# Attention with a gated feed-forward part: 70 products on a zero tile during the first loads, and another order of the first loads, splits and transposes

## What is computed

```python
xn = layernorm(x)                                  # over the last axis, no scale
s  = attn(xn)      # 16 heads of 128 over 4 key/value heads, causal softmax, output product,
                   # bias, gelu, + xn, layernorm with gamma and beta
gate_up = xn @ w_gate_up.T                         # 256 -> 2 x 1024
gate, up = split(gate_up, 2)
g  = silu((silu(gate) * up) @ w_down.T)            # 1024 -> 256
out = x + s * g
```

## Time and profile before

| | us |
|---|---|
| median of 3 runs | 727.29 |
| lowest, highest | 726.42, 732.52 |
| span of the profiled execution, from its first to its last instruction | 725.2 |

### The profile page before, as it was taken

The page is one execution under the profiler, slowest core; times in us unless marked ns, Lnnn a source line. Parts: engine busy times, 40 slices in busy tenths (PEclk is TensorE's granted clock), DMA queues, the critical chain, the costliest instruction groups (busy, mean ns, idle before and its releaser), DMA issues.

```text
span 725.2 us, 13208 instructions
## 1 busy us (share of the span) xinstructions
PE 679.8 (94%) x4032; PEld 594.3 (82%) x4032; DVE 493.0 (68%) x1636; ACT 428.5 (59%) x1011; POOL 280.1 (39%) x328
## 2 busy tenths in 40 slices
PE   2799999999899999999899999999999999999993
PEld 1678888888788888898788888887888898888872
DVE  6955433335777777778668677776777778867777
ACT  2423233326666667677667676866667677767671
POOL 2499100000523324157615142583324157615234
PEclk9699999999999999999999999999999999999998
DMA  8334000002000000000200000002000000200000
GB/s 273 116 117 145 1 29 0 30 0 88 1 1 2 1 1 1 1 1 1 91 2 1 2 1 1 2 4 89 1 1 1 1 1 1 88 1 2 0 1 30
DMA packets 14522, 20.52 MB, mean 28 GB/s; under 512 B 752, under 2 KB 12144, under 8 KB 14192
## 3 DMA queue, kind: packets, MB, share of 16 engines
q1 hardware_dynamic: 13328, 14.37, 6.0%
q0 software_dynamic: 1120, 5.24, 2.2%
HBM read 15.41 MB, written 4.19 MB: 27 GB/s over the span
## 4 chain that ended last, share of the span: by engine, by line
PE 84%; DVE 7%; ACT 3%; issue 3%; DMA 1%; SPq 0%; POOL 0%; DVEq 0%; ACTq 0%
PE bank L941 40%; PE down_ps L941 34%; PE down_ps L1028 8%; PE bank L1015 2%; DVE cT_lo L808 2%; ACT cT_hi L690 2%; DVE hidT_lo L754 1%; DMA raw<-in_wgu 1%; PE bank L994 1%; ACT probs L681 1%; DVE xnT_lo L739 1%; DVE pT_lo L792 1%; DVE xn L731 0%; DVE stats L716 0%; ACT wgu_hi L593 0%
## 5 line engine op out<-in xcount | busy, mean ns | idle before, releaser
L551 POOL TENSOR_TENSOR probs<-probs,inv 128x512 f32<-128x512 f32 (+3 forms) x256 | 181.1, 721 | 390.9 <-DVE inv L892 390.7
L681 ACT ACTIVATE probs<-probs,least 128x512 f32<-128x512 f32 (+3 forms) x256 | 142.4, 558 | 46.5 <-DVE least L885 45.0
L885 DVE CUSTOM_DVE_ANT_0 probs<-bank,mask 128x512 f32<-128x512 f32 (+3 forms) x256 | 121.4, 487 | 11.7 <-issue 11.2
L687 ACT ACTIVATE pT_hi<-down_ps 128x512 fp32r<-128x512 f32 x156 | 92.7, 594 | 49.1 <-PE down_ps L1028 41.8
L792 DVE TENSOR_TENSOR pT_lo<-down_ps,pT_hi 128x512 fp32r<-128x512 f32 x156 | 107.0, 686 | 17.4 <-ACT pT_hi L687 14.3
L1028 PE MATMUL down_ps<-ident,probs 128*128 128x128 f32 x624 | 93.5, 272 | 2.3 <-POOL probs L551 2.3
L1028 PEld LDWEIGHTS down_ps<-ident,probs 128*128 128x128 f32 x624 | 75.4, 140 | 14.8 <-POOL probs L551 2.5
L941 PE MATMUL down_ps<-wo_lo,cT_hi 128*128 128x256 f32 x256 | 73.5, 287 | 4.1 <-DVE cT_lo L808 3.0
L803 DVE SCALAR_TENSOR_TENSOR qT_lo<-bank,bias,qT_hi 128x512 fp32r<-128x512 f32 x64 | 47.7, 749 | 41.2 <-ACT qT_hi L671 41.2
L941 PE MATMUL bank<-kT_lo,qT_hi 128*128 128x512 f32 (+2 forms) x192 | 70.3, 366 | 2.4 <-issue 2.4
L941 PE MATMUL down_ps<-wo_hi,cT_lo 128*128 128x256 f32 x256 | 72.1, 282 | 0.0
(11 more groups left out here) (136 smaller groups left out, 1603.3 us busy)
## 6 DMA issues: line engine op xcount, KB each, us to landing
x_row<-in_x SPq DMA_DIRECT2D x4, 512.0 KB, 6.8
raw<-in_wgu SPq DMA_DIRECT2D x4, 512.0 KB, 6.0
raw<-in_wq POOLq DMA_DIRECT2D x2, 1024.0 KB, 5.2
raw<-in_wo POOLq DMA_DIRECT2D x2, 1024.0 KB, 6.4
g_scratch<-g_out SPq DMA_DIRECT2D x4, 512.0 KB, 2.9
x_b<-in_x SPq DMA_DIRECT2D x4, 512.0 KB, 3.6
g_b<-g_scratch SPq DMA_DIRECT2D x4, 512.0 KB, 4.6
out<-res SPq DMA_DIRECT2D x3, 512.0 KB, 3.5
```

The lines of the kernel that those rows point to most:

```text
L551: nc.gpsimd.tensor_tensor(p, p, inv[:, u % UNITS, g:g + 1].to_broadcast([P, (tile_of(u) + 1) * P]), ALU.mult).then_inc(probs_made, 1)
L681: nc.scalar.activation(p, p, ACT.Exp, bias=least[:, u % UNITS, g:g + 1], scale=-1.0, accum_out=total[:, u % UNITS, g:g + 1]).then_inc(exp_ ...
L687: nc.scalar.activation(hi[:], ps, ACT.Copy).then_inc(probsT_hi, 1)
L885: nc.vector.tensor_tensor_reduce(out=probs[t][:, g, :], in0=ps[:, 0:(t + 1) * P], in1=mask[:, (T - 1 - t) * P:], scale=-SCALE, scalar=BIG, ...
```

## The change

- TensorE: after a wait for a new zeroed tile `clock` (128x128 fp32r, a memset on VectorE), 70 matmuls of that tile with itself into the first 128 columns of bank 3. Nothing reads the result.
- SP: piece 0 of the gate/up weights and then the identity stand ahead of x of row 1.
- POOL: the low part of weight part 1 stands ahead of the root of row 1.
- ScalarE: silu of gate (0,0) stands ahead of the high parts of row 1.
- VectorE: the statistics of row 1 stand behind normalising row 0, the low part of weight part 0 and the low parts of row 0. The rest is in the order shown in the diff.
- TensorE: gate_up(0, 0) waits for the low parts of row 0 only, and stands ahead of the transposes of row 1. These now go to banks 1 and 3, and a wait for their low parts stands ahead of gate_up(0, 1).

```diff
+CLOCK_RUNS = 70
@@ build
+    clock = sb("clock", [P, P], F32R)
-    xT_ps = [flat[0:2], flat[2:4],
+    xT_ps = [flat[0:2], [flat[1], flat[3]],
              [down_ps[:, 0, :], down_ps[:, 1, :]], [down_ps[:, 2, :], down_ps[:, 3, :]]]
@@ sync
         load_tokens(0)
+        load_piece(0)
+        sp.dma_start(ident[:], ident_in).then_inc(ident_loaded, 16)
         load_tokens(1)
-        sp.dma_start(ident[:], ident_in).then_inc(ident_loaded, 16)
-        load_piece(0)
         load_tokens(2)
@@ gpsimd
         root1(0)
+        ffn_low(POOL_PARTS[0])
         root1(1)
-        ffn_low(POOL_PARTS[0])
         root1(2)
         root1(3)
@@ scalar
         ffn_high(0, 1)
         xT_high(0)
+        gate_part(0, 0)
         xT_high(1)
-        gate_part(0, 0)
         ffn_high(2, 3)
@@ vector
         nc.vector.memset(warm[:], 0.0).then_inc(table_warm, 1)
+        nc.vector.memset(f32(clock[:]), 0.0).then_inc(clock_tile, 1)
@@ vector
         mean_and_variance(0)
+        normalise(0)
+        ffn_low(DVE_PARTS[0])
+        xT_low(0)
         mean_and_variance(1)
-        normalise(0)
+        mean_and_variance(2)
         normalise(1)
-        xT_low(0)
-        ffn_low(DVE_PARTS[0])
+        normalise(2)
         xT_low(1)
-
-        mean_and_variance(2)
         mean_and_variance(3)
-        normalise(2)
+        hid_part(0, 0)
         normalise(3)
-        hid_part(0, 0)
         xT_low(2)
         xT_low(3)
@@ tensor
+        pe.wait_ge(clock_tile, 1)
+        for _ in range(CLOCK_RUNS):
+            nc.tensor.matmul(ring_ps[3][:, 0:P], clock[:], clock[:], start=True, stop=True)
         pe.wait_ge(ident_loaded, 16)
         transpose_tokens(0)
+        pe.wait_ge(xT_split, DC)
+        gate_up(0, 0, first=True)
         transpose_tokens(1)
         pe.wait_ge(xT_split, 2 * DC)
-        gate_up(0, 0, first=True)
         ffn_row(0, first=True)
```

More of the change, by code:

```diff
@@ L350, in build @@
         sem("out_made"), sem("out_stored"), sem("pool_chain"))
-    table_warm = sem("table_warm")
+    table_warm, clock_tile = sem("table_warm"), sem("clock_tile")
     tile_gelu, tile_var, tile_root, tile_normed, tile_chain_pool, tile_chain_dve, tile_out_pool, tile_out_dve, tile_scaled = (
```

## The result

| | before | after |
|---|---|---|
| median, us | 728.78 (4 runs, 726.42 to 732.52) | 740.58 (4 runs, 735.04 to 741.02) |
| span of the profiled execution | 725.2 | 739.0 |

The ratio is 1.0146, 95% interval 1.0105 to 1.0186: slower by 1.5%. The forecast was 729.7 and at most 733.0, with a chance of 0.11 for more than 1% slower.

The account below looks back on a forecast made before the run. VectorE's chain up to the first down product was taken as the bound, TensorE pacing the rest. Terms -0.15, +0.9, +0.65 and +1.0 gave +2.4 us: span 727.6, median 729.7, range 724.5 to 733.0.

Parts of the forecast that it names:

- The failing step: TensorE's 70 products at the start: clock rises after 5.5 us, so they run from 1.1 to 11.4.
- The bounds: Price of one 128x128 product: from half the transpose's 0.21 us up to plain f32, 0.22 high clock, 0.44 low.
- The sign of being wrong: Trace signs against the forecast: first down product before 30, products over 0.2 us apart, or gate_up(0,0) as late as 17.
- The rival with dear products: Products at the start cost 0.22 and 0.44 us each, run until 19.2; time 737.7; chance 0.10.
- The landing at 9.3: Gate/up weights, with less data loaded ahead, land at 9.3 instead of 11.05, 1.75 us earlier.
- POOL's half, "near 13.8": POOL's low part of the first gate/up weights ends near 13.8, so gate_up(0,0) starts near 14.1 instead of 17.8.
- VectorE as the chain, row 1's work moved behind: Before the first down product, row 1's 3.31 us on VectorE use up the landing's 1.75 us gain: -0.15 net.
- the products' 0.9: The 70 products delay row 0's transposes, so VectorE's low parts of row 0 end at 14.05, not 13.1: +0.9 us.
- the rival of the warm-up that does nothing: Clock falls again before gate_up(0,0), which ends at 19.2 instead of 16.9; time 730.6; chance 0.17.
- Row 3 held by POOL, 5.4 us: Before the first down product, POOL's wd low parts stretch xn of row 3 to 5.4 us instead of 1.38, as before.
- Transposes at the low clock: Row 3's transposes, ahead of the first down product, run at the low clock and uncovered: +1.0 us.
- If they slip against it, plus or minus 2 us: POOL's later attention-weight splits hold up hidT_lo; if they shift against VectorE's chain, the time varies by 2 us either way.

Follow-up runs that it names:

- The order alone: The changed kernel without its 70 products, everything else as changed: 730.1 us, ratio 1.0034 to the kernel before.
- POOL's wait: The changed kernel without its 70 products, POOL's two wd subtractions starting only when xn of row 3 is made: 731.5 us, ratio 1.0018.
- The products on ones: The changed kernel with its 70 128x128 products on a tile of ones instead of zeros: 735.6 us, one run.
- the cut: POOL's six attention-weight subtractions each cut into four: 731.7 us in the changed kernel; 723.2 us, ratio 0.9916, in the kernel before.
- the working warm-up: The changed kernel with 24 products of 128x512 (729.7 us, ratio 1.0036) or 40 of 128x256 (727.0 us, one run) instead of the 70.
- the kernel before with xn of row 3 first: The kernel before, POOL's two wd subtractions starting only when xn of row 3 is made: 725.5 us, ratio 0.9954.

## Why the prediction failed, step by step

- **The failing step: "So 5.5 us at 0.21 are 26 products, the other 44 take 4.8: the run ends at 11.4."** The price at the low clock was right (0.21). The rise was carried over from 512 wide products; the 128 wide ones had none. 70 x 0.21 = 14.8, end at 16.3. The bounds were drawn for the price of a product and not for whether the clock rises. Had the sum been made once without the rise, it would have given the measured end within 0.5 us; it lay 4.9 after the forecast one. Row 0's low parts ended at 19.4 instead of 14.05, 5.3 later, since the transposes too ran at the low clock (1.74 us in the chain); the first down product at 39.8, not 34.7, 5.1 later. Of the 11.4 us between the forecast span (727.6) and the measured one (739.0), 5.1 are this step; nearly all the rest lies behind that product (last item). The pieces from row 0's low parts to the first down product took 20.4 us in sum, against 20.65 in the forecast. One thing in between was off and did no harm: gate_up(0,0) was to run at the high clock and ran at the low one for its first 3.7 us, but VectorE's xn of row 1 came 0.3 us later still. The sign of being wrong, products more than 0.2 us apart, was named, and it came.
- **The rival with dear products** reached 19.2 by another road (0.22 and 0.44 a product). Its time of 737.7 was the nearest, by luck: its mechanism is not what happened, since at the low clock nothing above 0.21 was seen, and its sum has nothing for the stops that came later.
- **The landing at 9.3**: 9.50, and 7.9 to 9.3 in the other kernels with this order of loads. POOL's half, "near 13.8": 14.03. Right, hidden behind the products.
- **VectorE as the chain, row 1's work moved behind**: right. The order alone put the first down product at 34.0; the sum without the products' 0.9 gives 33.6. Missing was gate_up(0,0) at the low clock, named in the rival of the warm-up that does nothing, which held it hidden.
- **Row 3 held by POOL, 5.4 us**: 5.42, and 1.39 once POOL waits. (The Trainium skill, SBUF — State Buffer, "Who interferes with whom": between VectorE in a two-port mode and GpSimd, whoever issues first has the shared ports for its whole instruction. By that rule the trace agrees where POOL goes first; with POOL's wait the two don't overlap at this place, so VectorE going first isn't shown by it.) **Transposes at the low clock**: 1.98 us for 8, right.
- **"If they slip against it, plus or minus 2 us"** for POOL's later splits: mis-sized. The first hidT_lo that met a long subtraction (55.92) came 0.44 us after POOL began (55.48), in the old kernel 0.84. That small shift made TensorE's stop longer (2.04 instead of 1.65), the clock fell behind it, and later chunks slid into later subtractions: 5.5 us by 94 us. The term left out the clock behind a stop.

The products on ones are a second trace of the same schedule, and show the other case. Their first down product is at 39.78, like the changed kernel's, but the low clock lasted longer behind it: to the next down product it was 6.62 us instead of 6.11. So hidT_lo came 0.98 us after POOL began, later and not earlier, and TensorE's stop was 1.52:

```profile
55.45 4.60 POOL L507 TENSOR_TENSOR wq_lo<-raw,wq_hi 128x2048 fp32r<-128x2048 f32 x1
...
56.43 4.18 DVE L757 TENSOR_TENSOR hidT_lo<-hid,hidT_hi 128x512 fp32r<-128x512 f32 x1 [0.70 <-ACT hidT_hi L608]
60.75 0.36 PE L943 MATMUL down_ps<-wd_lo,hidT_hi 128*128 128x256 f32 x1 [1.52 <-DVE hidT_lo L757]
...
88.39 1.43 PE down_ps L943 x12
```

The clock stayed high, and the chunk that the changed kernel reached at 93.86 came at 88.39, 7.7 us later than before the change (80.71): as much as at the first down product. This run took 735.6. One of the changed kernel's four took 735.0, which fits, but has no trace. So the 5.5 us hang on 0.5 us at 56 us and need not come in every execution; the 7.7 are the change's. The shift was not set on purpose in any run. That the stops come from long subtractions is shown by the cut.

## What to carry to other kernels

A warm-up must be made of the kind of products that were seen to raise the clock, and its length must be bounded by the case that the clock does not rise, ahead of work that waits behind it in the same queue. Ask first whether the warm engine is on the chain there: here even the working warm-up moved the first down product by 0.8 to 1.9 us at most, and the times show nothing of it. Where VectorE and POOL both work from SBUF, cut POOL's instructions into short ones: it bought 0.8%, more than any reordering here, and narrowed the spread of the times (3.2 us over 10 runs, against 9.1 over 31).

## What the runs showed of the hardware that I had not expected

- 15.2 us of gapless 128x128 fp32r products with TensorE busy all the time stayed at 1.2 GHz, with zeros and with ones; 256 and 512 wide ones, on zeros, rose to 2.4 GHz after 4 and 3 us.
- At 1.2 GHz an fp32r product of 128 columns takes 0.21 us, as long as one of 256.
- The profile's clock column says 1.00 during all of this. In this case a stretch of low clock at the start shows only in the durations: 330 ns for a weight load, 187 when the clock is high; 415 ns for a 256 wide product, 278 when it is high.
- A stop of TensorE of 2.04 us was followed by the low clock (low from 61.0), one of 2.48 too, but 1.2 us after its end (low from 84.8). The stops of at most 1.66 us behind the first down product left it up in every trace here. Length alone doesn't tell: with 512 wide products a stop of 2.83 us, ahead of 12.9 us, left it up, and so did one of 2.48 (ahead of 73.1) in the kernel before with xn of row 3 first.
